# The second expert layer: from all experts for every token to sorted tiles in two groups

## The reference, cut to what matters

```python
logits = (x @ wt.T + repeat(g @ wg.T)) / 2
scores = softmax(logits)                        # 8 experts
topk_w, topk_idx = top_k(scores, 2)
topk_w = topk_w / (topk_w.sum(-1) + 1e-20)
gp = leaky(einsum('th,ehm->etm', x, w_gate))    # m = 128
up = einsum('th,ehm->etm', x, w_up)
y_all = einsum('etm,emh->eth', gp * up, w_down)
y = (y_all[topk_idx, t] * topk_w).sum(1)
y = y + (leaky(x @ sw_gate) * (x @ sw_up)) @ sw_down    # shared, 256 wide
```

## Time and profile before

| | |
|---|---|
| time, median of 3 runs | 2637.17 us (2636.77 to 2638.17) |
| the profiled execution's own time | 2626.76 us |
| its span | 2624.7 us |
| TensorE busy | 2493.8 us (95%) |
| VectorE busy | 1415.8 us (54%) |
| ScalarE busy | 1076.7 us (41%) |
| POOL busy | 994.2 us (38%) |
| second expert layer, from its first instruction to the end | 377.0 us of the span |

### The profile page before, as it was taken

The page is one execution under the profiler, slowest core; times in us unless marked ns, Lnnn a source line. Parts: engine busy times, 40 slices in busy tenths (PEclk is TensorE's granted clock), DMA queues, the critical chain, the costliest instruction groups (busy, mean ns, idle before and its releaser), DMA issues. The chain is left out here.

```text
span 2624.7 us, 38034 instructions
## 1 busy us (share of the span) xinstructions
PE 2493.8 (95%) x13330; PEld 1555.2 (59%) x13330; DVE 1415.8 (54%) x3290; ACT 1076.7 (41%) x2635; POOL 994.2 (38%) x1037
## 2 busy tenths in 40 slices
PE   7999999899999899899999999999999899899998
PEld 4565655533444367686868787555656566444456
DVE  7475665467777353533323243565565678455555
ACT  4767586344544324111111111565566355112122
POOL 3665565168778334641212121864654200000000
PEclk9999999889999989999999999999999999999997
DMA  4000000000000045500000100432333000400000
GB/s 162 1 1 1 1 1 21 9 13 13 13 9 13 2 147 167 180 1 1 0 1 0 43 1 23 135 121 82 100 115 95 0 1 1 132 0 3 3 11 26
DMA packets 91518, 108.52 MB, mean 41 GB/s; under 512 B 16396, under 2 KB 72597, under 8 KB 91078
## 3 DMA queue, kind: packets, MB, share of 16 engines
q1 hardware_dynamic: 87606, 96.27, 11.6%
q0 software_dynamic: 3728, 9.83, 1.3%
HBM read 92.52 MB, written 9.35 MB: 39 GB/s over the span
## 5 line engine op out<-in xcount | busy, mean ns | idle before, releaser
L1014 POOL TENSOR_TENSOR cb_sc<-cb_toep,cb_mk 128x128 f32<-128x128 f32 (+3 forms) x256 | 215.9, 872 | 188.5 <-ACT cb_pr L1052 179.0
L1014 POOL TENSOR_TENSOR cb_bias<-cb_bias,cb_mk 128x128 f32<-128x128 f32 (+3 forms) x256 | 215.1, 872 | 147.1 <-DMA cb_bias<-in_fside_16xSxS 146.7
L1653 DVE TENSOR_REDUCE gb_bmax<-PS 128x8 f32<-128x512 f32 x256 | 164.3, 684 | 87.4 <-PE PS L1431 87.1
L398 PE MATMUL PS<-ident,cb_pr 128*128 128x128 f32 x1280 | 198.3, 284 | 4.0 <-ACT cb_pr L1052 2.3
L699 DVE CUSTOM_DVE_ANT_0 cb_sc<-PS,cb_sc,cb_sneg 128x128 f32<-128x128 f32 (+3 forms) x256 | 129.8, 546 | 122.0 <-PE PS L388 118.5
L398 PEld LDWEIGHTS PS<-ident,cb_pr 128*128 128x128 f32 x1280 | 135.0, 141 | 96.3 <-issue 81.9
L1812 ACT ACTIVATE gb_pt<-PS 128x512 f32<-128x512 f32 x256 | 139.3, 596 | 111.1 <-PE PS L1438 106.0
L1431 PE MATMUL PS<-gb_ks,gb_qs 32*128 32x512 f32 x512 | 171.5, 670 | 8.4 <-DVE gb_bmax L1653 6.8
L1058 ACT ACTIVATE cb_pt<-PS 128x128 f32<-128x128 f32 (+3 forms) x448 | 163.3, 414 | 38.0 <-PE PS L398 37.6
L699 DVE CUSTOM_DVE_ANT_0 cb_bias<-PS,cb_bias,cb_sneg 128x128 f32<-128x128 f32 (+3 forms) x256 | 129.1, 545 | 89.9 <-PE PS L388 88.9
L2379 PE MATMUL PS<-eb_g,ff_h 128*128 128x256 f32 x768 | 173.6, 379 | 0.0
(11 more groups left out here) (669 smaller groups left out, 5160.9 us busy)
## 6 DMA issues: line engine op xcount, KB each, us to landing
cb_bias<-in_fside_16xSxS SPq DMA_DIRECT2D x64, 256.0 KB, 2.9
cb_bias<-in_fside_16xSxS SPq DMA_DIRECT2D x64, 192.0 KB, 2.5
ff_h<-in_L_ffn_h_w SPq DMA_DIRECT2D x2, 4096.0 KB, 15.5
cb_bias<-in_fside_16xSxS SPq DMA_DIRECT2D x64, 128.0 KB, 2.2
y_rows<-eb_g SPq DMA_DIRECT2D x19, 256.0 KB, 2.2
cb_toep<-rel_table SPq DMA_DIRECT2D x8, 512.0 KB, 6.7
cb_bias<-in_fside_16xSxS SPq DMA_DIRECT2D x64, 64.0 KB, 2.3
ff_w<-in_L_ffn_w_w SPq DMA_DIRECT2D x3, 1024.0 KB, 8.3
```

The source lines that it names most:

```text
L398: ins = pe.transpose(PS[:, bank, j * P:j * P + P], pr[:, v % 2, e, j * P:j * P + P], ident)
L1014: ins = pool.tensor_tensor(biases(v, e), turned(h, n) if L0 else biases(v, e), mk[:, b % 2, packed(t):packed(t) + n], ALU.add)
L1653: dve.tensor_reduce(bmax[:, n % 2, t, g + e, 0:NB], PS[:, bank + e, :].rearrange("p (n k) -> p n k", k=64), AX.X, ALU.max)\
```

## The change

`expert_layer` is replaced by `second_experts`. It sorts as the first layer does, but in two groups of two batches, each of 2 x 8 + 8 - 1 = 23 tiles (12 pairs, the last of one tile). The shared experts of batches 0 and 1 come before group 0, those of 2 and 3 between the groups. The routing of group 1 stands between the pairs of group 0, on VectorE, and the first steps of the token stages of batches 0 and 1 between the pairs of group 1. All else of the token stages follows the last pair, in one list. y now has tokens on the partitions (in `Y`), so `rows` goes, and `turn_y` with two copies on ScalarE makes the turned form for `token_weights`. `choice(b)` now waits for `chosen_mask(b - 2)`, as `hot` exists twice. Other steps of the token stage are the same. Copies of the turned products (`copy_hidden`) move to ScalarE; pairs have one bank each for rows, hidden and output. Buffers for stores are two.

```diff
+GB = B // 2
+GJ = GB * NT
+GT = 2 * GJ + NE - 1
+GP = (GT + 1) // 2
+YS2 = 2
...
+        turned, logit, routing, pair_x, pair_in, pair_h, pair_y = (
+            Turns(sm, uses, k) for k in ((6, 7), (5,), (6, 7), (0,), (1, 2), (3,), (4,)))
+        gates, ups, back, mixed, late = (Turns(sm, uses, k) for k in ((1, 2), (3, 4), (0, 5), (5, 6, 7), (0, 1, 2, 3, 4, 5, 6, 7)))
...
+                def tiles(grp, i):
+                    if 1 <= i and i + 1 < GP:
+                        turn_rows(grp, i + 1)
+                    if i < GP:
+                        pair_into(grp, i)
+                    if i == 0:
+                        turn_rows(grp, 1)
+                    if i + 1 < GP:
+                        expert_of(grp, i + 1)
+                    if 1 <= i <= GP:
+                        turn_hidden(grp, i - 1)
+                    if i >= 2:
+                        pair_out(grp, i - 2)
...
+                turn_x(0)
                 cond_logits()
+                turn_x(1)
                 logits(0)
+                into(0, 0)
+                logits(1)
+                into(0, 1)
+                turn_x(2)
+                logits(2)
+                into(1, 0)
+                down(0)
+                ranks(0)
+                turn_x(3)
+                logits(3)
+                into(1, 1)
+                rows_of_slots(0)
+                down(1)
+                pe.wait_ge(sm["mo_routed"], 16 * 5)
+                expert_of(0, 0)
+                turn_rows(0, 0)
+                for i in range(GP + 1):
+                    tiles(0, i)
+                    if i == 3:
+                        ranks(1)
+                    elif i == 8:
+                        rows_of_slots(1)
+                into(2, 0)
+                pair_out(0, GP - 1)
+                into(2, 1)
+                into(3, 0)
+                down(2)
+                into(3, 1)
+                expert_of(1, 0)
+                turn_rows(1, 0)
+                down(3)
+                for i in range(GP + 1):
+                    tiles(1, i)
+                    if i == 2:
+                        turn_y(mixed, 0)
+                    elif i == 3:
+                        token_weights(mixed, 0)
+                    elif i == 7:
+                        chosen_rows(mixed, 0)
+                        turn_choice(mixed, 0)
+                    elif i == 9:
+                        turn_normed(mixed, 0, 0)
+                        turn_y(mixed, 1)
+                    elif i == 10:
+                        queries_keys(mixed, 0)
+                        token_values(mixed, 0)
+                    elif i == 11:
+                        token_weights(mixed, 1)
+                turn_queries(mixed, 0)
+                pair_out(1, GP - 1)
+                mask_columns(mixed, 0)
+                chosen_mask(mixed, 0)
+                token_scores(mixed, 0, 0)
...
+                turn_mixed(late, 1)
+                token_out(late, 1)
+                turn_normed(late, 1, 1)
+                hidden(late, 1)
+                chosen_rows(late, 2)
...
+                def combine(b, ts):
+                    grp = b // GB
+                    for k in range(2):
+                        for t in ts:
+                            j, m = b * NT + t, k * NT + t
+                            dve.wait_ge(dyn[f"yg_in{b % 2 * YG + m}"], 16 * yg_turn(b))
+                            if t % 2 == 0:
+                                back.wait_emptied(dve, (b, t // 2))
+                            ins = dve.scalar_tensor_tensor(out=Y[:, j, 0:D], in0=yg[:, b % 2 * YG + m, :],
+                                                           scalar=w12[:, grp, k, j - grp * GJ:j - grp * GJ + 1], in1=Y[:, j, 0:D],
+                                                           op0=ALU.mult, op1=ALU.add)
...
+                token_weights(1)
+                own_weights()
+                token_scores(0)
+                for t in range(NT):
+                    count(1, t)
+                choice(1)
+                mix_values(0)
+                chosen_rows(1)
+                rms(1, 0)
+                normed(1, 0)
+                token_out(0)
+                rms(0, 1)
+                turn_normed(1, 0)
+                normed(0, 1)
+                combine(2, range(NT))
...
+                gather(0, range(GT))
+                routing.wait_emptied(pool, ("rows", 1))
+                gather(1, range(XG))
+                pool.wait_ge(sm["mo_slots"], 2)
+                stored(0)
+                return_rows(0)
+                gather(1, range(XG, 2 * XG))
+                return_rows(1)
+                gather(1, range(2 * XG, GT))
+                rows_of_mask(0)
+                stored(1)
+                return_rows(2)
+                return_rows(3)
+                rows_of_mask(1)
+                rows_of_mask(2)
+                rows_of_mask(3)
```

More of the change, by code:

```diff
@@ L1964 @@
 G = 64
-CR = 32 + NE
 DF = 1024
 FC = DF // P
[L1972 to L1977, removed]
 def load_small(sp, a, small, sm):
@@ new lines, in tensor_program @@
+                queries_keys(late, 1)
+                token_values(late, 1)
+                turn_normed(late, 0, 1)
+                hidden(late, 0)
+                turn_queries(late, 1)
+                mask_columns(late, 1)
+                processed(late, 0)
+                chosen_mask(late, 1)
+                token_scores(late, 1, 0)
+                token_scores(late, 1, 1)
+                turn_y(late, 2)
+                back_to_rows(late, 0)
+                token_weights(late, 2)
@@ new lines, in tensor_program @@
+                token_values(late, 3)
+                token_out(late, 2)
+                turn_queries(late, 3)
+                mask_columns(late, 3)
+                turn_normed(late, 2, 1)
+                hidden(late, 2)
+                chosen_mask(late, 3)
+                token_scores(late, 3, 0)
+                token_scores(late, 3, 1)
+                processed(late, 2)
+                turn_probabilities(late, 3)
+                back_to_rows(late, 2)
+                mix_values(late, 3)
@@ new lines, in vector_program @@
+                rope(1)
+                processed(0)
+                token_scores(1)
+                kept_rows(0)
+                back_to_rows(0)
+                token_weights(2)
+                own_weights()
+                combine(3, range(NT))
+                mix_values(1)
+                for t in range(NT):
+                    count(2, t)
+                choice(2)
+                token_out(1)
+                rms(1, 1)
+                normed(1, 1)
+                turn_normed(1, 1)
@@ new lines, in vector_program @@
+                chosen_rows(2)
+                rms(2, 0)
+                normed(2, 0)
+                token_weights(3)
+                own_weights()
+                processed(1)
+                turn_normed(2, 0)
+                kept_rows(1)
+                back_to_rows(1)
+                rope(2)
+                for t in range(NT):
+                    count(3, t)
+                choice(3)
+                token_scores(2)
+                chosen_rows(3)
+                rms(3, 0)
+                normed(3, 0)
```

1558 lines of the change are left out of this document (664 added, 894 removed).

## The result

| | before | changed |
|---|---|---|
| median (13 runs each) | 2635.81 us (2627.34 to 2639.53) | 2622.77 us (2615.44 to 2644.36, and one of 3136.89) |
| span of the profiled execution | 2624.7 us | 2617.0 us |
| second expert layer | 377.0 us | 363.7 us |

The ratio is 0.996, 95% interval 0.9944 to 0.9976; the medians lie 13.0 us apart. The execution of 3136.89 us was a slow one, at a mean clock of 0.73, and is not in the ratio. The forecast was 66 us faster; the time lies above its range of 2545 to 2606 us. The sign was right, the size was not.

The account below looks back on a forecast made before the run. TensorE was taken to bound the second expert layer, busy 357.9 of 377.0 us. Groups ending at +163 plus a tail of 148 gave 311, 66 less; 2637.17 - 66 = 2571 us, range 2545 to 2606.

Parts of the forecast that it names:

- The sign: Whole kernel: faster at 0.95, within 0.2% at 0.01, slower at 0.04.
- part 3, the tail: After the last pair, rest of batch 0 and token stages of batches 1 to 3: 148 us, before 77.0.
- the low clock: Rival, chance 0.12: TensorE stays at 1.2 GHz through the tail, up to 40 us more, 2611 us.
- the walk: Tail followed through the three queues' written orders: batches done at +42, +76, +125 and +154 us.
- the ratio on VectorE's work: Tail: 73 us of VectorE work at 1.47 us per us is 107, plus 27 for the last chain: 134 us.
- Part 1: Second expert layer up to its first tile: +46 us, bounds 40 and 53.
- Part 2: The two groups of tiles with shared experts between: from +46 to +163 us of the layer, bounds -4 and +12.
- wrong if group 1 takes over 60 us: Test on group 1, forecast from +111 to +163 us: over 60 us would mean its interleaved work stalls it.
- The return of rows: Gathers in POOL's queue after the last pair: no cost, with 5 us of cover for batch 1's mask.
- Better overlap: Rival, chance 0.13: the tail costs 1.25 us per us of VectorE's work, so 118 us, 2541 us.
- no overlap: Rival, chance 0.05: the four token stages do not overlap, tail 219 us, layer 5 us longer, 2642 us.
- the 50 of the test: Tail: forecast wrong if one batch's return comes over 50 us after the other's.

Follow-up runs that it names:

- the combined kernel: Changed kernel with batch 3's shared experts in the tail, batch 2's chosen rows ahead of hidden of batch 1, and 18 idle matmuls: 0.9839, 2579.23 us.
- the repeat: The changed kernel run again with nothing edited, first of three such series, without stalls: 0.9901 of the kernel before, median 2595.14 us.
- the 10.5 us gap: Changed kernel with batch 2's chosen rows and their turn ahead of hidden of batch 1, where VectorE stood idle: 0.9882, tail 170.5 us.
- the four traces: Traces of the changed kernel, unedited, from its first series and three more: 0.996, 0.9901, 0.9967 and 0.9865 of the kernel before.
- the third repeat: The changed kernel run again with nothing edited, in the last of three more series, without stalls: 0.9865 of the kernel before.
- the finely cut kernel: Changed kernel with idle matmuls of 64 columns ahead of 32 waits of the tail: 1.0109 of the kernel before, tail 235.4 us.
- the one experiment meant for it: Changed kernel with at most 4 tiles of rows of x fetched ahead instead of 8, second layer only: 0.9952 of the kernel before.

## Why the prediction was wrong

**The step that failed is part 3, the tail.** I walked the queues with durations from rows at the full clock, counted on a clock above 0.8, and put the low clock aside as a rival at 0.12 because 48.1 us of mixed work had run at 0.95. The tail ran at 0.69. In the changed kernel's tail `hidden` (16 matmuls, two rows each) and the last `processed` were:

```profile
2476.27 4.94 PE L3418 MATMUL PS<-eb_hnT,rw_w 128*128 128x63 f32 x32 [0.66 <-DVE eb_hnT L3791]
...
2516.87 7.06 PE L3418 MATMUL PS<-eb_hnT,rw_w 128*128 128x63 f32 x32 [0.66 <-DVE eb_hnT L3791]
...
2567.63 7.06 PE L3418 MATMUL PS<-eb_hnT,rw_w 128*128 128x63 f32 x32 [0.66 <-DVE eb_hnT L3791]
...
2594.44 7.06 PE L3418 MATMUL PS<-eb_hnT,rw_w 128*128 128x63 f32 x32 [0.66 <-DVE eb_hnT L3791]
2602.27 6.62 PE L3426 MATMUL PS<-rw_w,eb_g 128*63 128x256 f32 x16 [0.77 <-ACT eb_g L4152]
```

At the full clock they are, in the combined kernel:

```profile
2556.62 3.75 PE L3418 MATMUL PS<-eb_hnT,rw_w 128*128 128x63 f32 x32 [0.66 <-DVE eb_hnT L3802]
2561.15 3.64 PE L3426 MATMUL PS<-rw_w,eb_g 128*63 128x256 f32 x16 [0.77 <-ACT eb_g L4165]
```

The chain of waits through the tail, of the repeat, by line:

```profile
by line: PE PS L3418 15.5%; PE PS L3426 11.9%; PE PS L3395 7.1%; DVE eb_junk L3730 6.7%; PE PS L3345 5.2%; issue 4.5%; PE PS L3304 4.1%; PE PS L3438 3.4%; PE PS L3409 2.4%; DVE eb_sT L3818 2.3%; PE PS L3383 2.1%; DVE eb_mxs L3823 2.1%; PE P
```

Of its 170.2 us the pieces on TensorE make about 106, those on VectorE about 45. `hidden` (L3418), `processed` (L3426) and `mix_values` (L3395) are 34.5% of it, 58.7 us; at their full-clock lengths (3.75, 3.64 and 1.98 in the combined kernel, four times each) they would be 37.5, 21 us less. They are not all: by the trace's record of the clock, 72 of TensorE's 106 us in the chain stood at 1.2 GHz, so at the full clock the same pieces would be some 36 us shorter. This is an estimate, and more than the miss. Other waits would take back a part of it, how much no run shows; what the runs won back is 4.8 to 10 us.

The ends of the batches say where the walk was lost. VectorE's last addition of each (L3862):

```profile
2494.22 1.29 DVE L3862 TENSOR_TENSOR sel_Y<-sel_Y,PS 128x512 f32<-128x512 f32 x2
...
2536.02 1.29 DVE L3862 TENSOR_TENSOR sel_Y<-sel_Y,PS 128x512 f32<-128x512 f32 x2
...
2585.66 0.69 DVE L3862 TENSOR_TENSOR sel_Y<-sel_Y,PS 128x512 f32<-128x512 f32 x1 [0.17 <-PE PS L3438]
...
2611.89 0.69 DVE L3862 TENSOR_TENSOR sel_Y<-sel_Y,PS 128x512 f32<-128x512 f32 x1 [0.17 <-PE PS L3438]
```

They end at +49, +91, +140 and +166 us of the tail, its last store at +170.5; the walk had +42, +76, +125 and +154. So at least 15 us were lost with batches 0 and 1. From there to batch 2 it took 49 us, as in the walk, and to batch 3 26 us where the walk had 29, though the clock was 0.72 and 0.63 there, no higher than in the first two (0.72 and 0.67). As the matmuls ran long there too, something else in the walk was too long; what it is isn't shown.

So of the 22.5 us of miss in the tail, 6 are not the walk's: it ended at 154, and I took 148 because the ratio on VectorE's work said 134. Of the other 16.5, the low clock is the failed term as far as is known: runs show 4.8 to 10 us of it, and the rest stays open. The rival of the low clock was priced at up to 40 us for all of the tail. The old mixed stretch was a denser one, TensorE busy 43.6 of 48.1 us, against 125.2 of 170.5 here; the last stretch of the kernel before, 20.85 of 28.9 at 0.62, was the nearer one.

The Trainium skill's page "TensorE: Matmul & The Clock Gate" (Part 1, "What's actually happening") says that throttling is the default and activity lifts it. The trace agrees in the direction: idle matmuls took the tail from 0.69 to 0.85.

**VectorE's work was no measure by itself.** It was forecast well (79, measured 82). But its price was 0.55 us per us where half the count was left out, and the 10.5 us gap was worth nothing. That the ratio and the walk agreed (134 and 154) was no support, as both rested on TensorE at or near its full speed (0.95 in the stretch of the ratio).

**Part 1** (46): 47.5, 53.2, 47.8 and 49.5 us in the four traces. In the longest TensorE was busy 46.12 us at a clock of 0.78, in the first 40.04 at 0.89, 6.1 more, and that is the difference of 5.7. From the longest, logits and the first expert:

```profile
2244.42 3.42 PE L3180 MATMUL PS<-ex_wt,eb_xT 128*128 128x8 f32 x16
2247.69 6.64 PE L3190 MATMUL PS<-eb_xT,eb_room 128*128 128x512 f32 x8
```

The first takes 1.85 us at the full clock, the second 3.69 in the third repeat.

**Part 2.** Pairs that nothing disturbed started 3.25 us apart, as forecast. Group 0 with the shared experts took 69.1 us without stalls (forecast 65), group 1 56.6 (52), so 4 and 5 us more. With the stalls: 79.0 and 66.7. Those 20 us no row of before held, since its trace was one without them. My test "wrong if group 1 takes over 60 us (then its interleaved work stalls it)" tripped, but not for that reason: without the stalls it took 56.6 with the interleaved work.

**The return of rows** held: GpSimd had the gathers of the two batches issued, and `rows_of_mask(1)` started 24.4 us after the last pair (forecast 25); TensorE did not wait for it.

```profile
2449.49 0.98 POOL L4268 DMA_INDIRECT eb_yg<-y_group,eb_slot_at  x1 [19.29 <-issue]
...
2470.91 1.83 POOL L4276 DMA_INDIRECT eb_M<-in_L_ffn_attention_mask,eb_index  x1 [0.30 <-issue]
```

```profile
2482.05 0.63 PE L3312 MATMUL PS<-ident,eb_M 63*128 63x63 f32 x4
```

**The other rivals.** Better overlap and no overlap did not come; one batch was done at most 49.0 us after the other, just under the 50 of the test.

The 52.7 us of miss in the layer are thus 22.5 in the tail, 20 of stalls in the two groups (by the first repeat), 8.7 that the groups take without them, and 1.5 in part 1. The profiled spans differ by 7.7 us only, the layers by 13.3: the first layer's tiles had the stalls in this execution (70.1 us) and not in that of before (62.4).

## What to carry to other kernels

When dense work is taken off TensorE, price what remains at both clock levels: the sparse remainder may be the place where the clock falls, and then matmuls that were short stand in the chain at twice their length. Before an idle gap of one engine is worth an edit, look at what that engine waits for next: here the gap moved a few instructions on. When work is moved, compare all parts of the layer and not its total: 4.9 of the 6.5 us that moving one batch's shared experts seemed to win lay in a part that the edit doesn't touch. And ask of a trace which kind of execution it shows before its rows price a phase that is to be doubled.

## What the hardware showed unexpectedly

- Two stretches of idle matmuls in the finely cut kernel, both without a gap on TensorE. In the first the clock was 0.53, so nearly all of it at 1.2 GHz; in the second, 66 us on, it was 1.00. Why is open:

```profile
2428.40:2446.30 17.90, 17.90 (x89) 17.78 (x89) 8.66 (x21) 1.05 (x1) 13.94 (x14) 0.53 0.33 97
...
2494.80:2507.00 12.20, 12.20 (x110) 12.20 (x111) 4.25 (x10) 0.61 (x2) 0.00 (x0) 1.00 0.06 21
```

- With less work on TensorE its clock was lower still, 0.61 for 0.69, and of some 23 us left out only 10.1 came off its busy time.
- The stalls: in phases of tiles with indirect DMAs, ScalarE and GpSimd start some 5 to 7 us late, together (the longest waits of ScalarE in the first layer's tiles are 5.1 to 6.6 us, without stalls 2.7), in every trace of three series and in none of three others, one chip being in both. The seven traces with them hold no landing of the 153 indirect DMAs, the twelve of the changed kernel and its edits without them 142 to 153. Their cause stays open; the one experiment meant for it fell in a series without them.
